# Three instead of two PSUM banks for each score tile in the attention stage of a transformer layer on eight cores

## The reference

```python
q, k, v = x @ Wq.T + bq, x @ Wk.T + bk, x @ Wv.T + bv      # heads of 64
scores = einsum('bqhd,bkhd->bhqk', q, k) * 64 ** -0.5
scores = scores * exp(-alpha * abs(i - j))                  # decay by lag
attn = softmax(scores)
x = layernorm(x + einsum('bhqk,bkhd->bqhd', attn, v) @ Wo.T + bo)
h = silu(fp4(x) @ fp4(Wg).T) * (fp4(x) @ fp4(Wu).T)         # fp4(): blocks of 16 along the row are
x = layernorm(x + fp4(h) @ fp4(Wd).T)                       # scaled to 6, rounded to 8 levels, scaled back
```

## Time and profile before

| what | us |
|---|---|
| median of 2 runs | 3305.03 (3298.46 to 3311.61) |
| the profiled execution's own time | 3300.35 |
| its span, core 0, the slowest | 3298.8 |
| spans of the 8 cores | 3253.6 to 3298.8 |
| DVE busy in the span | 2228.2 |
| PE busy in the span | 1610.1 |

### The profile page before, as it was taken

One profiled execution on the slowest core, in us unless ns is written; L12 is line 12 of the kernel. 1 busy time (PEld: TensorE's weight loads), 2 busy tenths in 40 slices (PEclk: granted clock), 3 DMA queues, 4 the chain that ended last, 5 costly groups with the idle time before them and its releaser, 6 DMA issues.

```text
span 3298.8 us, 26073 instructions; the slowest of 8 cores (3253.6 to 3298.8 us)
## 1 busy us (share of the span) xinstructions
PE 1610.1 (49%) x7186; PEld 555.5 (17%) x7186; DVE 2228.2 (68%) x3256; ACT 979.5 (30%) x892; POOL 33.1 (1%) x53
## 2 busy tenths in 40 slices
PE   5887555455554555555550010000027667663298
PEld 2332111111111111111220000000013223221143
DVE  2002877778777777777358878888867888888323
ACT  1112444444444444444351111111112222222022
POOL 0000000000000000000000000000000000000000
PEclk9777556666667666666785555555558888887599
DMA  5110000000000000000251111111100111111344
GB/s 77 26 26 18 18 23 18 22 18 22 18 22 18 20 15 20 16 13 10 72 181 43 40 51 38 39 38 39 38 13 18 38 39 39 45 39 39 114 170 160
DMA packets 91551, 141.19 MB, mean 43 GB/s; under 512 B 59666, under 2 KB 59666, under 8 KB 91410
## 3 DMA queue, kind: packets, MB, share of 16 engines
q1 hardware_dynamic: 76290, 90.76, 8.9%
q0 software_dynamic: 10512, 31.99, 3.8%
q10 hardware_dynamic: 4608, 16.78, 1.3%
HBM read 104.35 MB, written 36.18 MB: 43 GB/s over the span
## 4 chain that ended last, share of the span: by engine, by line
DVE 49%; PE 21%; issue 14%; ACT 8%; DMA 6%; DVEq 1%; SPq 1%; ACTq 0%; POOL 0%; POOLq 0%
DVE SDr L524 13%; ACT PT L536 5%; PE ps_o L922 5%; PE ps_q L328 4%; DVE qc L188 4%; DVE qxn L158 4%; DVE qr L151 4%; PE ps_av L472 2%; PE ps_q L348 2%; DVE qc L178 2%; DVE qm L183 2%; DVE qc L185 2%; DVE qc L160 2%; PE ps_tp L216 2%; DVE qm L173 2%
## 5 line engine op out<-in xcount | busy, mean ns | idle before, releaser
L524 DVE TENSOR_TENSOR SDr<-ps_s,Wd 128x512 f32<-128x512 f32 x1024 | 641.2, 682 | 337.9 <-PE ps_s L498 253.2
L536 ACT ACTIVATE PT<-SDr 128x2048 bf16<-128x2048 f32 x256 | 474.9, 1902 | 474.4 <-DVE SDr L524 426.9
L498 PE MATMUL ps_s<-QT,KT 64*128 64x512 bf16 x1024 | 269.1, 514 | 378.2 <-DVE SDr L524 371.6
L472 PE MATMUL ps_av<-PT,VV 128*64 128x512 bf16 x1024 | 281.3, 541 | 244.5 <-DVE QT L562 244.5
L164 ACT ACTIVATE qcc<-qc 128x1024 bf16<-128x1024 bf16 (+1 forms) x84 | 99.0, 1179 | 882.5 <-DVE qc L160 882.5
L816 PE MATMUL ps_g<-wgT,x1qT 128*128 128x512 bf16 (+1 forms) x768 | 213.6, 432 | 181.0 <-DVE hbuf L835 180.3
L479 PE MATMUL ps_d<-PT,ones 128*64 128x512 bf16 x1024 | 276.4, 531 | 0.0
L216 PE MATMUL ps_tp<-idn,wqo 128*128 128x128 bf16 x352 | 51.4, 291 | 459.6 <-DVE wqo L189 430.8
L498 PEld LDWEIGHTS ps_s<-QT,KT 64*128 64x128 bf16 x1024 | 62.5, 98 | 724.8 <-issue 724.8
L822 PE MATMUL ps_u<-wuT,x1qT 128*128 128x512 bf16 (+1 forms) x768 | 184.4, 387 | 0.0
L922 PE MATMUL ps_o<-wdT,hin 128*128 128x512 bf16 x704 | 154.9, 384 | 2.0 <-DMA x1in<-x_scr 2.0
(11 more groups left out here) (110 smaller groups left out, 2121.2 us busy)
## 6 DMA issues: line engine op xcount, KB each, us to landing
awst<-wd SPq DMA_DIRECT2D x16, 704.0 KB
wst<-wu SPq DMA_DIRECT2D x11, 1024.0 KB
hqT_scr<-hqT POOLq DMA_DIRECT2D x16, 704.0 KB, 3.4
hin<-hqT_scr SPq DMA_DIRECT2D x16, 704.0 KB
xres<-x SPq DMA_DIRECT2D x16, 512.0 KB, 4.1
x_scr<-ra ACTq DMA_DIRECT2D x16, 512.0 KB, 2.8
x1sl<-x_scr SPq DMA_DIRECT2D x8, 1024.0 KB
x1in<-x_scr SPq DMA_DIRECT2D x16, 512.0 KB
```

What stands on the lines that cost most here:

```text
L472: p.do("tensor", lambda e, kt=kt, PT=PT, rq0=rq0, h=h: e.matmul(out=ps_av.ap()[rq0:rq0 + 64, :], lhsT=VVa[:, kt, h * 64:(h + 1) * 64], rhs ...
L498: e.matmul(out=ps.ap()[:, b2 * 512:b2 * 512 + QC], lhsT=KTa[rq0:rq0 + 64, hp, kt * 128:(kt + 1) * 128], rhs=QTa[rq0:rq0 + 64, hp, qc * QC: ...
L524: return e.tensor_tensor(out=SDr.ap()[:, s8 * 512:(s8 + 1) * 512], in0=ps.ap()[:, b2 * 512:b2 * 512 + QC], in1=wd_ap, op=ALU.mult)
L536: e.activation(out=PT.ap()[:, 4 * g * QC:(4 * g + 4) * QC], in_=SDr.ap()[:, r8 * 2048:(r8 + 1) * 2048], func=AF.Exp), sA, 1)
```

## The change

`ps_s1` and `ps_s2` get three banks each, and step kt writes bank kt % 3. PE therefore waits before the scores of step kt for the pair of step kt - 3, and no longer for that of kt - 2. With 16 steps in a unit the count starts anew at 0: steps 15 and 0 of the next unit have the same bank, so there PE waits for the pair just before. All 8 banks of PSUM are then in use.

```diff
-                 nc.psum_tensor("ps_s1", [128, 2 * 512], F32) as ps_s1, \
-                 nc.psum_tensor("ps_s2", [128, 2 * 512], F32) as ps_s2, \
+                 nc.psum_tensor("ps_s1", [128, 3 * 512], F32) as ps_s1, \
+                 nc.psum_tensor("ps_s2", [128, 3 * 512], F32) as ps_s2, \
...
-                sd_kt = {0: 0, 1: 0}
+                sd_kt = {0: 0, 1: 0, 2: 0}
...
-                            b2 = kt % 2
+                            b2 = kt % 3
```

## The result

| what | before | after |
|---|---|---|
| median of the comparison's runs, us | 3273.26 (30 runs) | 3237.72 (31 runs) |
| ratio, 95% interval | | 0.9906, 0.9882 to 0.993 |
| own time of the profiled execution, us | 3300.35 | 3237.32 |
| spans of the 8 cores, us | 3253.6 to 3298.8 | 3227.7 to 3235.8 |
| attention stage, us | 1302.7 | 1266.3 |

The change makes the kernel about 0.9% faster, within 2%; the quotient of the two medians, 0.989, lies inside the interval. Of both kernels some executions take about 30 us longer than the rest, with a lower granted TensorE clock on some cores, and the two runs and the profile of before that were shown ahead are of these.

A forecast was written before the change was run, and what follows sets the result against it. DVE was taken to bound the attention stage, its idle time being what counts. 36 - 2 - 1 = 33 us less than 3300.35 gave 3267, put at 3270 between two bases; own range 3258 to 3280, stated range 3256 to 3303.

The forecast's parts named there:

- Steps 1 to 3: DVE's attention-stage loss to two banks: 24.2 us in 57 listed waits, 5 broken overlap, 7 short gaps; about 36.
- Steps 2 and 3: Attention stage: waits breaking the overlap of DVE's pairs, 5 us, and gaps too short to be listed, some 7 us.
- Step 4: Stretches without quantization: with three banks a 0.46 us wait remains at the sixth pair, in about 5 of 20; 2 us stay.
- Step 5: Bank shared by steps 15 and 0: hidden at unit ends, costs 1 us once, from unit 0 to unit 1.
- Step 6: Other lateness in attention: ACT keeps up with 1 us to spare; the wait before L562 (5.44 us) moves along unchanged.
- The third bank is full when a stretch begins: Least known assumption, taken as full since PE stands 2.85 us there and a group takes 1.54; never full would gain nothing.
- A: Rival: third bank of half use, quantization groups too close or ACT's ring a wait; gain about 16 us, 3284; chance 0.18.
- B: Rival: third bank of no use, DVE's waits depend on PE's rate alone; 3300 us; chance 0.09.
- C: Rival: PE's clock stays at 1.2 GHz in the stretches; 24 stretches lose 61 us, 25 slower, 3325; chance 0.05.
- The 60 waits that the change can't touch: DVE's waits before the first pairs after unit ends, 54.1 us, laid to PE's in-order list; no free bank helps.

## Why the prediction was right and where it was wrong

**The step that failed** is the base of the sum: "against the profiled execution's own time 3300.35: 3267. The median of the two runs shown lies 5 us above that execution, so I put the forecast between the two bases: 3270." The gain was right and what it was taken from was not. On core 0 of that execution the attention stage begins at 308.4 us, on cores 2 to 7 at 264.7 to 275.1. The kernel before, run again, begins it at 271.6 to 276.9 everywhere and takes 3276.81; its median over 30 runs is 3273.26. Taking the same 33 us from these gives 3240 to 3244, and 3237.72 was measured. The earlier trace rows held the warning: the eight spans run from 3253.6 to 3298.8, so the slowest core was 45 us behind the fastest with equal work. The range covered the unknown of the change, and not that of the base. The prediction also took 2% for about what can be told from no change; the interval measured over some 30 runs of each, 0.9882 to 0.993, shows that 1% can.

**Steps 1 to 3, the loss to two banks.** 57 listed waits of 24.2 us, 5 us of broken overlap, 7 of short gaps. The stage is 36.4 us shorter. Listed waits on groups give 20.5 of that, where 24.2 less the 3 of steps 4 and 5 were forecast. DVE's busy time gives 10.2 (pairs that no longer stand alone), and 5.9 is left, with 0.2 taken off by the wait before L562. Of these 5.9, six listed waits before pairs that are gone make up 2.1 (four on ACT's exponentials, L536, 1.4, and two without a cause named, 0.7); the rest are gaps that no row lists. Steps 2 and 3 had 12 for these 16, so they were sized somewhat low. Five pairs in a row take 6.05 to 6.07 where 6.05 was worked out. That the loss hangs on the distance of the wait is shown by the run that keeps three banks and the old distance.

**Step 4, what stays.** 0.46 in about 5 stretches was forecast, 2 us. Six waits of 0.22 to 0.24 stayed, 1.4 us; in the stretch that was worked out it is the sixth pair's, as forecast (419.23).

**Step 5, the shared bank.** Hidden at the unit ends, as forecast: numbering the banks on gives about 1.4 us in all. From unit 0 to unit 1 the first pair waits 1.94, where about 1.8 was forecast.

**Step 6, what is late next.** The wait before L562 stayed at 159 us, and ACT's ring did not turn into a wait: the four waits of 1.4 us on it that stood before are gone.

**The third bank is full when a stretch begins.** Yes, where it was looked at: the five pairs from 412.93 run unbroken, and PE stood for 2.85 us before the scores at 414.36. Over the stage PE waits 431.6 us for DVE, where it waited 371.6.

**The rivals.** A would have left the stage at about 1286, B at 1302; neither. C's price counts 24 stretches where step 4 counts 20. C wanted the clock down in the stretches; the stage's mean was 0.65 before and 0.66 after. In the stretch from 412.93 the clock rises with three banks as it did with two (core 3, columns as in the earlier trace rows):

```profile
414.30:419.50 5.20, 5.14 (x20) 1.02 (x20) 4.96 (x9) 4.07 (x3) 0.54 (x1) 0.51 0.18 69
419.50:424.00 4.50, 2.39 (x18) 0.62 (x16) 4.50 (x8) 3.35 (x2) 0.00 (x0) 1.00 0.00 0
```

The Trainium skill's section "A second HAM failure mode: psum-queue depth-cycling" (page "TensorE: Matmul & The Clock Gate") has the clock oscillate when PE cycles through banks and idles briefly between groups. The traces agree that it goes back and forth, with two banks and with three; a loss by the third bank, which C expected, they don't show.

**The 60 waits that the change can't touch.** Right for the bank, but the prediction took PE's order alone as the cause. The experiments show a second one: the pair waited for four matmuls that it doesn't need. Once it waits for the scores alone, 37 us of the stage go, and the third bank is worth 9. PE's order keeps the rest, 25.0 us in 45 waits.

## What to carry to other kernels

Before a sum is taken from one profiled execution, compare the spans of all cores, and the stages ahead of the change and behind it: a core that loses time there shifts the base by as much as a small change gives. A further buffer gives one step of lead, and it paid here in the stretches in which the producer was slower than the consumer. First look whether a wait counts work that the waiting instruction doesn't need: taking that out gave 63 us here, and left the third bank 9 of its 35. The order of the work was worth more here than the buffer: with the scores issued ahead and DVE's pairs put into a wait for a third engine, the kernel was 3.1% faster than before with two banks and 4.2% with three, against 0.9% for the third bank alone.

## What the runs showed of the hardware

Without any lead (one bank) the granted clock stayed at 0.50, the level of 1.2 GHz, for the whole stage (290 to 2200 us): where no quantization part stood between, each group of some 1.6 us was followed by a pause as long. With two banks it went from 0.50 to 0.99 within a stretch, with three from 0.51 to 1.00. And the same program's projection stage ran at a granted clock from 0.76 to 0.92, different from core to core of one execution, while the attention stage, which DVE bounds, took the same time within 3.5 us at all of them.
